# One transfer for all but the last 392 nodes, issued behind the last load, and the last group's remainder rows first

## The chip, the cores and the metric

The kernel runs on one core of a Trainium2 chip. Its time is device microseconds (us), a median over runs. An execution taken by the hardware profiler gives the span (first to last instruction) and the trace. TensorE is PE, VectorE is DVE, ScalarE is ACT, GpSimd is POOL, SyncE is SP. Transfers issued by SP run as queue q1 and those issued by ACT as queue q10. One trace shows both on the core's 16 DMA engines. KB is 1024 bytes, MB and GB are powers of ten.

## What is computed

One layer over 5000 nodes with 64 features, float32:

```python
h = jnp.maximum(_layernorm(x, axis=-1), 0.0)
neighbors = adj @ h                                   # adj is 5000 x 5000
neighbors = neighbors / (num_neighbors[:, None] + 1e-7)
out = jnp.concatenate([h, neighbors], axis=-1) @ fc_w.T + fc_b
return x + relu(out)
```

The 5000 x 5000 matrix is 100 MB and every element of it is read once.

## The kernel before

The host gives the kernel adj transposed, with its columns (the nodes whose sums are wanted) in three groups of 2048, 2560 and 392. `GROUPS` holds them as (first block of 512, blocks, first accumulator). The kernel multiplies h by the neighbour half of `fc_w` first, which gives `g_sb` (128 rows x 40 tiles x 64), so that the big product is g^T times a tile of adj: 64 output rows on one half of the TensorE array, and two halves side by side.

Contraction runs over 5000 source nodes: 39 tiles of 128, and a remainder of 8 rows (`REM`). For each group in turn, `LOADS` lists the transfers of 1 to 4 tiles each, 40 in all. SP issues them in that order into a ring `raw` of 128 x 32768 floats, and waits on `load_used` before it reuses a place. TensorE takes tile after tile in `multiply` (line 611) and accumulates into the banks of the group: `acc[0]`, `acc[1]` for the group of 2048, `acc[2]` to `acc[4]` for that of 2560, and the bank `turned` (which is `acc[5]`) for the last 392 columns. A place in this order is written (group, tile).

The 8 remainder rows of a group are loaded by ACT into `adj_rem`, every 16th lane (`REM_STEP`), and multiplied in `remainder` (line 624) behind the tile that `REM_AFTER` names. Lanes between them hold zeros from a memset on GpSimd (line 279). The first group's rows are loaded early; those of the second wait for `rem_used` of the first and are issued at 116.6 us; those of the last group wait for the second's.

When a group is summed, VectorE scales its banks by 1/neighbours (`scale`, `scale_alone`), TensorE flips them back to nodes x features in `flip` at the places of `FLIP_AFTER`, into the two banks `y[0]` and `y[1]`, and VectorE adds what h contributes by itself and then x (`finish`). `out_ready` counts the banks finished. The last 392 nodes have a shorter way: `preload_self` (line 647, behind tile (2, 25)) puts their own part into `y[0]` and `y[1]` by a product with the identity, once `out_ready` is 5. Behind the last tile come `scale_last`, `flip_last` (line 653), which adds to the same banks, and `finish_last` (line 526).

There are three stores of the output. ACT issues the one of the first group (512 KB, pieces of 1 KB) when `out_ready` is 2, and the one of the second (640 KB, pieces of 1.25 KB) when it is 5 (line 358). SP issues the one of the last 392 nodes (98 KB, line 268) behind all loads, when `out_ready` is 6. A piece is what lies together in memory: a lane of `out_sb` holds 36 nodes that are neighbours in the output, and a group takes 4 or 5 out of each 9 of them. The kernel ends when both engines have seen their stores land.

Of the kernel before, what the change touches and what calls it, by code (L numbers as in the profile page):

```python
# [18 lines left out]

LANDINGS = 24  # L20

REM_STEP = 16
REM_GAP = 8
LN_EPS = 1e-5
DIV_EPS = 1e-7
# [14 lines left out]
def gnn_layer(nc, x, adj_groups, num_neighbors, fc_t, fc_b, out):  # L40
# [64 lines left out]
    TURN_AFTER = {(0, 3): 1, (0, 7): 2, (0, 13): 3, (0, 21): 4}  # L105
    WEIGH_AFTER = {(0, 5): 1, (0, 11): 2, (0, 19): 3, (0, 27): 4}
    SPREAD_AFTER = (0, 38)
    REM_AFTER = {(0, 33): 0, (1, 11): 1, (2, 3): 2}
    FLIP_AFTER = {(1, 7): 0, (1, 9): 1, (2, 9): 2, (2, 13): 3, (2, 17): 4}
    PRELOAD_AFTER = (2, 25)  # L110
    LN_OPS = 8

    REM_LOADS = [sum(1 + (w > BLOCK and w % (2 * BLOCK) > 0) for w in WIDTH[:g + 1]) for g in range(G)]

    with ExitStack() as ctx:
        def sb(name, shape, dt=F32):
# [9 lines left out]
        g_sb = sb("g_sb", [LANES, TILES, F])  # L126
        cen = sb("cen", [LANES, BT * F])
        h_pairs = [sb(f"h_pairs{i}", [LANES, BT * F]) for i in range(2)]
        ht = [sb(f"ht{i}", [LANES, BLOCK]) for i in range(2)]
        ht_rows = sb("ht_rows", [LANES, 2 * SIDE])  # L130
        ht_rem = sb("ht_rem", [LANES, LANES])
# [33 lines left out]
        bias_copied = sem("bias_copied")  # L165
        landed = [sem(f"landed{k}") for k in range(LANDINGS)]
        rem_loaded = sem("rem_loaded")
        ln_dve = sem("ln_dve")
        ln_act = sem("ln_act")
        ident_cleared = sem("ident_cleared")  # L170
# [30 lines left out]
        def nodes(v, m0, m1):  # L201

            return v[0:TAIL0, :].rearrange("(p i m) f -> p i (m f)", i=RUN, m=FULL)[:, :, m0 * F:m1 * F]

        def tail(v):

# [34 lines left out]
        @block.sync  # L241
        def _(sp):
            def load(n):
                g, m, i0, i1 = LOADS[n]
                w = WIDTH[g]
                if loads_before(n):
                    sp.wait_ge(load_used, loads_before(n))
                r = RUN if m < FULL else TAIL_RUN
                rows = adj_groups[g][m * BLOCK:m * BLOCK + r * LANES, 0:w].rearrange("(p i) c -> p (i c)", i=r)
                sp.dma_start(raw[:, place(n):place_end(n)], rows[:, i0 * w:i1 * w]).then_inc(loaded(n)[0], 16)  # L250

            def load_x(k):
# [36 lines left out]
        def _(act):  # L289
            def load_rem(g):  # L290
                w = WIDTH[g]
                if g:
                    act.wait_ge(rem_used, g)
                else:
                    act.wait_ge(rem_cleared, 2)
                rows = adj_groups[g][REM0:N, 0:w]
                lanes = slice(0, REM * REM_STEP, REM_STEP)
                k = w // (2 * BLOCK) * 2
                if k:
                    act.dma_start(adj_rem[lanes, 0:k, 0:BLOCK],  # L300
                                  rows[:, 0:k * BLOCK].rearrange("r (k c) -> r k c", k=k)).then_inc(rem_loaded, 16)
                if w > k * BLOCK:
                    act.dma_start(halves(adj_rem[lanes, k, :])[:, :, 0:(w - k * BLOCK) // 2],
                                  rows[:, k * BLOCK:w].rearrange("r (s c) -> r s c", s=2)).then_inc(rem_loaded, 16)

            def load_few():

# [47 lines left out]
            def store(g):  # L355
                m0, m1 = GROUPS[g][0], GROUPS[g + 1][0]
                act.wait_ge(out_ready, banks(g)[-1] + 1)
                act.dma_start(nodes(out, m0, m1), blocks(out_sb, m0, m1)).then_inc(stored, 16)


            act.wait_ge(warm_ready, 1)
            nc.scalar.activation(std[:, 0:1], warm[:], ACT.Sqrt)
# [13 lines left out]
            for b in range(SETS):  # L376
                copy_spread(b)
            load_rem(1)
            store(0)
            load_rem(2)  # L380
            store(1)
            act.wait_ge(stored, 32)

        @block.vector
        def _(dve):
# [46 lines left out]
            def add_bias(b):  # L432
                if b == 0:
                    dve.wait_ge(bias_spread, 1)
                    nc.vector.tensor_copy(bias[:], acc[ALONE][:, 0:F]).then_inc(bias_copied, 1)
# [86 lines left out]
            def finish_last():  # L522

                for i in range(2):
                    dve.wait_ge(flipped, LAST + i + 1)
                    done = nc.vector.scalar_tensor_tensor(
                        tail_half(out_sb, i), y[i][0:LAST_LANES, 0:2 * F].rearrange("p (s f) -> p s f", s=2), 0.0,
                        tail_half(x_sb, i), ALU.max, ALU.add)
                done.then_inc(out_ready, 1)

# [26 lines left out]
        def _(pe):  # L557
# [47 lines left out]
            def multiply(n, i):  # L605
# [3 lines left out]
                for b in banks(g):  # L609
                    for s, c0, width in sides(g, b):  # L610
                        last = nc.tensor.matmul(acc[b][s * HALF:(s + 1) * HALF, 0:width], g_sb[:, t, :],  # L611
                                                raw[:, c + c0:c + c0 + width], start=t == 0, stop=t == CH - 1,
                                                tile_position=(0, s * HALF))
                if i == i1 - 1:
                    last.then_inc(load_used, 1)

            def remainder(g):
                pe.wait_ge(rem_loaded, 16 * REM_LOADS[g])
                for b in banks(g):
                    for s, c0, width in sides(g, b):  # L620
                        k = adj_rem[:, c0 // BLOCK, 0:BLOCK]
                        if width < BLOCK:
                            k = halves(adj_rem[:, (c0 - s * width) // BLOCK, :])[:, s, 0:width]
                        last = nc.tensor.matmul(acc[b][s * HALF:(s + 1) * HALF, 0:width], g_sb[:, CH, :], k,  # L624
                                                start=False, stop=False, tile_position=(0, s * HALF))
                last.then_inc(rem_used, 1)

            def flip(b):
# [13 lines left out]

            def preload_self():

                pe.wait_ge(out_ready, LAST)
                for i in range(2):
                    nc.tensor.matmul(y[i][0:LAST_LANES, 0:2 * F].rearrange("p (s f) -> p s f", s=2),
                                     ident[0:LAST_LANES, 0:LAST_LANES], tail_half(out_sb, i), start=True, stop=False)

            def flip_last():  # L650
                for i in range(2):
                    pe.wait_ge(scaled, LAST + i + 1)
                    nc.tensor.matmul(y[i][0:LAST_LANES, 0:2 * F], sums[0][:, i * LAST_LANES:(i + 1) * LAST_LANES],
                                     ident[:], start=False, stop=True).then_inc(flipped, 1)


            pe.wait_ge(bias_loaded, 16)
            pe.wait_ge(bias_cleared, 2)
            nc.tensor.matmul(acc[ALONE][:, 0:F], ones[:], bias_row[:], start=True, stop=True).then_inc(bias_spread, 1)  # L659
            pe.wait_ge(ident_ready, 1)  # L660
            turn(0)
            pe.wait_ge(weights_loaded, 32)
# [53 lines left out]
```

## Time and profile before

| | |
|---|---|
| time, median of 3 runs | 250.93 us (250.77 to 251.14) |
| profiled execution: its own time | 250.9 us |
| profiled execution: its span | 249.1 us |
| PE busy | 207.5 us (83%) |
| DVE, ACT, POOL busy | 41.3, 15.2, 3.7 us |
| DMA, bytes and mean rate | 102.79 MB, 413 GB/s |
| mean granted clock of TensorE | 0.959 |

The profiled execution's time is 1.8 us above its span; that part lies around the instructions. In the rows below a share of DMA time is a share of 16 engines for the length of the window: 10% of a window of 8 us is 0.8 us in which all 16 would be taken. A matmul in float32 counts as two instructions on TensorE, so a tile of the first group has 8, one of the second 12, one of the last 4.

### The profile page before, as it was taken

To read this page: it belongs to the slowest core of one execution; us is meant where nothing else is said; L and a number is where in the kernel's file an instruction comes from. 1 tells how busy PE (TensorE), PEld (TensorE's weight loads), DVE (VectorE), ACT (ScalarE), POOL (GpSimd) and SP (SyncE) were. 2 spreads that over 40 slices of the span, in tenths; PEclk is the share of its full clock that TensorE was granted. 3 is DMA by queue.
4 is the path that set the end of the run, shared out by engine and by line. 5 is a ranking of instruction groups with operands and counts; after the bars stand their busy time and mean duration, and the time that the engine had idled before them with its cause. 6 is when DMAs were issued, how large, how long until landed. Compare 5 with 4: busy or idle time off the path is not lost.

```text
span 249.1 us, 2445 instructions
## 1 busy us (share of the span) xinstructions
PE 207.5 (83%) x1084; PEld 86.2 (35%) x1084; DVE 41.3 (17%) x101; ACT 15.2 (6%) x35; POOL 3.7 (1%) x13
## 2 busy tenths in 40 slices
PE   0279899688997997998995299997398998798994
PEld 0143333322432442332332033332132433235782
DVE  1762333330020050006002001000000000003411
ACT  2130220120020010003000000000000000000000
POOL 5000000000000000000000000000000000000000
PEclk9999999997999999999999579999769999999999
DMA  8999999999999999999999999999999999999992
GB/s 294 411 431 421 427 421 421 432 424 414 418 426 453 437 442 389 441 428 431 399 429 441 441 434 400 430 457 431 434 431 407 424 424 424 421 415 417 417 395 71
DMA packets 8309, 102.79 MB, mean 413 GB/s; under 512 B 1412, under 2 KB 3244, under 8 KB 4972
## 3 DMA queue, kind: packets, MB, share of 16 engines
q1 hardware_dynamic: 6754, 101.29, 96.1%
q10 hardware_dynamic: 1546, 1.36, 1.6%
q8 instruction: 8, 0.13, 0.2%
q14 instruction: 1, 0.01, 0.0%
HBM read 101.37 MB, written 1.28 MB: 412 GB/s over the span
## 4 chain that ended last, share of the span: by engine, by line
DMA 66%; PE 29%; DVE 2%; ACT 1%; SPq 1%; issue 1%
DMA raw<-adj_group 64%; PE acc L611 24%; DMA x_sb<-x 2%; PE acc L624 2%; PE y L576 2%; PE turned L611 1%; SPq L250 1%; PE turned L564 0%; DVE cen L426 0%; DVE cen L414 0%; DVE var L418 0%; DVE mean L407 0%; ACT g_sb L348 0%; ACT sums L322 0%; ACT ht L342 0%
## 5 line engine op out<-in xcount | busy, mean ns | idle before, releaser
L611 PE MATMUL acc<-raw,g_sb 128*64 128x512 f32 (+1 forms) x780 | 162.8, 573 | 25.3 <-DMA raw<-adj_group 24.4
L611 PEld LDWEIGHTS acc<-raw,g_sb 128*64 128x64 f32 x780 | 56.5, 142 | 125.2 <-issue 90.2
L492 DVE TENSOR_TENSOR sums<-acc,rnn_bc 128x512 f32<-128x512 f32 x4 | 2.6, 686 | 78.6 <-PE acc L611 76.6
L611 PE MATMUL turned<-raw,g_sb 128*64 128x196 f32 x156 | 14.8, 334 | 0.9 <-DMA raw<-adj_group 0.8
L576 PE MATMUL y<-w_both,ht 128*128 128x256 f32 (+1 forms) x40 | 12.1, 440 | 0.8 <-ACT ht L342 0.8
L611 PEld LDWEIGHTS turned<-raw,g_sb 128*64 128x64 f32 x156 | 10.5, 136 | 4.2 <-DMA raw<-adj_group 2.1
L442 DVE TENSOR_TENSOR out_sb<-y,bias 128x128 f32<-128x128 f32 x20 | 4.4, 284 | 38.2 <-ACT g_sb L348 38.2
L576 PEld LDWEIGHTS y<-w_both,ht 128*128 128x128 f32 x40 | 8.0, 217 | 5.6 <-issue 4.4
L518 DVE TENSOR_TENSOR out_sb<-y,out_sb 128x512 f32<-128x512 f32 (+1 forms) x5 | 3.2, 639 | 33.9 <-PE y L637 32.8
L463 DVE TENSOR_TENSOR rnn_diag<-ident,rnn 128x512 f32<-128x512 f32 x8 | 5.0, 686 | 19.6 <-PE y L601 19.6
L564 PE MATMUL turned<-ident,h_pairs 128*128 128x128 f32 x20 | 3.7, 315 | 4.6 <-DVE h_pairs L430 4.6
L418 DVE TENSOR_REDUCE var<-sums 128x8 f32<-128x512 f32 x5 | 3.4, 686 | 16.3 <-ACT sums L322 16.3
L659 PE MATMUL acc<-bias_row,ones 128*128 128x64 f32 x2 | 0.7, 448 | 6.2 <-DMA bias_row<-fc_b 6.2
L348 ACT ACTIVATE g_sb<-y 128x256 f32<-128x256 f32 x10 | 3.3, 381 | 41.2 <-PE y L576 26.3
L601 PE MATMUL y<-rnn_diag,ones 128*64 128x512 f32 (+1 forms) x20 | 4.6, 552 | 0.8 <-ACT rnn_bc L353 0.7
L564 PEld LDWEIGHTS turned<-ident,h_pairs 128*128 128x128 f32 x20 | 2.4, 156 | 8.0 <-issue 7.2
L353 ACT ACTIVATE rnn_bc<-y 128x512 f32<-128x512 f32 (+1 forms) x5 | 2.9, 587 | 25.1 <-PE y L601 25.1
L407 DVE TENSOR_REDUCE mean<-x_sb 128x8 f32<-128x512 f32 (+1 forms) x6 | 3.5, 590 | 4.9 <-DMA x_sb<-x 4.9
L624 PE MATMUL acc<-adj_rem,g_sb 128*64 128x512 f32 (+1 forms) x20 | 4.2, 550 | 0.0
L342 ACT ACTIVATE ht<-turned 128x512 f32<-128x512 f32 x5 | 3.0, 597 | 19.5 <-PE turned L564 19.5
L414 DVE TENSOR_TENSOR cen<-x_sb,mean 128x512 f32<-128x512 f32 (+1 forms) x6 | 3.5, 602 | 0.2
L322 ACT ACTIVATE sums<-cen 128x512 f32<-128x512 f32 x5 | 3.1, 626 | 7.0 <-DVE cen L414 6.0
(56 smaller groups left out, 41.3 us busy)
## 6 DMA issues: line engine op xcount, KB each, us to landing
raw<-adj_group SPq DMA_DIRECT2D x9, 4096.0 KB, 31.8
raw<-adj_group SPq DMA_DIRECT2D x5, 5120.0 KB, 26.7
raw<-adj_group SPq DMA_DIRECT2D x8, 2560.0 KB, 27.6
raw<-adj_group SPq DMA_DIRECT2D x7, 784.0 KB, 27.3
raw<-adj_group SPq DMA_DIRECT2D x3, 1280.0 KB, 21.2
raw<-adj_group SPq DMA_DIRECT2D x1, 3072.0 KB, 28.3
raw<-adj_group SPq DMA_DIRECT2D x4, 392.0 KB, 19.1
x_sb<-x SPq DMA_DIRECT2D x2, 576.0 KB, 4.7
```

The lines of the kernel that those rows point to most:

```text
L348: nc.scalar.activation(to[:, 2 * k:2 * k + 2, :, :], weighed_parts(k, 1), ACT.Copy).then_inc(g_copied, 1)
L407: last = nc.vector.tensor_reduce(narrow(mean[:]), rows, AX_X, ALU.add)
L414: last = nc.vector.tensor_tensor(wide(cen[:]), rows, m.unsqueeze(len(m.shape)).to_broadcast(list(rows.shape)), ALU.subtract)
L418: nc.vector.tensor_reduce(var[:], sums[0][:].rearrange("p (t f) -> p t f", f=F), AX_X, ALU.add).then_inc(ln_dve, 1)
L442: last = nc.vector.tensor_tensor(to[:, 2 * k:2 * k + 2, :], weighed_parts(k, 0)[:, :, s, :], bias[:].unsqueeze(1).to_broadcast([LANES, 2, ...
L463: last = nc.vector.tensor_tensor(split(to[:, s, :]), ident[:].unsqueeze(1).to_broadcast(shape), rnn[:, m + s:ROWS:FULL].unsqueeze(2).to_br ...
L518: nc.vector.tensor_tensor(o, split(y[b % 2][:, 0:RUN * F * (m1 - m0)]), o, ALU.add).then_inc(summed, 1)
L564: last = nc.tensor.transpose(turned[:, c], h_pairs[b % 2][:, c], ident[:])
L576: last = nc.tensor.matmul(weighed_tiles(i)[:, 0:w], ht[b % 2][:, c:c + LANES], flat(w_both[:])[:, 0:w], start=True, stop=True)
L601: last = nc.tensor.matmul(y[b % 2][k, c], ones[:, 0:HALF], r, start=True, stop=True, tile_position=(0, s * HALF))
L611: last = nc.tensor.matmul(acc[b][s * HALF:(s + 1) * HALF, 0:width], g_sb[:, t, :], raw[:, c + c0:c + c0 + width], start=t == 0, stop=t == ...
L624: last = nc.tensor.matmul(acc[b][s * HALF:(s + 1) * HALF, 0:width], g_sb[:, CH, :], k, start=False, stop=False, tile_position=(0, s * HALF))
```

## The change

The two stores on ACT become one on SP, issued behind the last load when `out_ready` is 5: 1152 KB, in which each lane is one piece of 9216 bytes. The store of the last 392 nodes goes from SP to ACT. The remainder rows of the last group get a tile of their own (`adj_rem_last`, which is `h_pairs[1]` after its last use, cleared on GpSimd), are loaded by ACT right behind those of the second group, and are multiplied behind tile (1, 23), where they open the accumulation; the first tile of the last group then adds to it. `preload_self` goes from tile (2, 25) to (1, 19), waits for the scaling of the first group's two banks, and writes `acc[0]` and `acc[1]` in place of `y[0]` and `y[1]`; `flip_last` and `finish_last` use these too. The remainder rows lie in every 4th lane. The bias is spread through `acc[SETS - 1]`, which is the same bank as before (`ALONE` is 4 and `SETS` is 5).

```diff
-REM_STEP = 16
+REM_STEP = 4
...
-    REM_AFTER = {(0, 33): 0, (1, 11): 1, (2, 3): 2}
+    REM_AFTER = {(0, 33): 0, (1, 11): 1, (1, 23): 2}
...
-    PRELOAD_AFTER = (2, 25)
+    PRELOAD_AFTER = (1, 19)
...
+        adj_rem_last = h_pairs[1]
...
-            sp.wait_ge(out_ready, LAST + 1)
-            sp.dma_start(tail_nodes(out), tail(out_sb)).then_inc(last_stored, 16)
-            sp.wait_ge(last_stored, 16)
+
+            sp.wait_ge(out_ready, LAST)
+            sp.dma_start(out[0:TAIL0, :].rearrange("(p r) f -> p (r f)", r=ROWS), flat(out_sb[:, 0:ROWS, :])
+                         ).then_inc(stored, 16)
+            sp.wait_ge(stored, 16)
...
+            pool.wait_ge(ones_ready, 3)
+            pool.wait_ge(turned_done, SETS - 1)
+            nc.gpsimd.memset(adj_rem_last[:], 0.0).then_inc(rem_cleared, 1)
...
                 if g:
-                    act.wait_ge(rem_used, g)
+                    act.wait_ge(rem_used, 1)
...
+                if g == 1:
+                    act.wait_ge(rem_cleared, 3)
+                    act.dma_start(halves(adj_rem_last[lanes, :])[:, :, 0:SIDE],
+                                  adj_groups[G - 1][REM0:N, :].rearrange("r (s c) -> r s c", s=2)).then_inc(rem_last_loaded, 16)
...
             load_rem(1)
-            store(0)
-            load_rem(2)
-            store(1)
-            act.wait_ge(stored, 32)
+            act.wait_ge(out_ready, LAST + 1)
+            act.dma_start(tail_nodes(out), tail(out_sb)).then_inc(last_stored, 16)
+            act.wait_ge(last_stored, 16)
...
-                                                raw[:, c + c0:c + c0 + width], start=t == 0, stop=t == CH - 1,
+                                                raw[:, c + c0:c + c0 + width], start=g < G - 1 and t == 0, stop=t == CH - 1,
...
             def preload_self():
 
-                pe.wait_ge(out_ready, LAST)
+                pe.wait_ge(scaled, 2)
                 for i in range(2):
-                    nc.tensor.matmul(y[i][0:LAST_LANES, 0:2 * F].rearrange("p (s f) -> p s f", s=2),
+                    nc.tensor.matmul(acc[i][0:LAST_LANES, 0:2 * F].rearrange("p (s f) -> p s f", s=2),
                                      ident[0:LAST_LANES, 0:LAST_LANES], tail_half(out_sb, i), start=True, stop=False)
```

## Rows read from the trace of the kernel before

**Rows 1.** The page, parts 2 and 3: busy tenths in 40 slices; the DMA queues.

```profile
DMA  8999999999999999999999999999999999999992
...
q1 hardware_dynamic: 6754, 101.29, 96.1%
q10 hardware_dynamic: 1546, 1.36, 1.6%
```

**Rows 2.** The chain of waits from 200 us to the end: start us, us, what.

```profile
224.86 2.37 PE acc L611 x12
...
229.35 15.57 DMA raw<-adj_group
...
244.97 0.58 PE turned L611 x4
...
246.38 0.51 DVE out_sb L526 x2
```

**Rows 3.** DMA queues, 195 to 236 us, no store under way.

```profile
DMA packets 1853, 17.33 MB, mean 423 GB/s; under 512 B 207, under 2 KB 207, under 8 KB 1080
```

**Rows 4.** DMA queues, 150.7 to 192.4 us, the first store: issue KB, us to landing.

```profile
q10 hardware_dynamic: 546, 0.53, 3.7%
...
out<-out_sb ACTq DMA_DIRECT2D x1, 512.0 KB, 41.6
```

**Rows 5.** DMA queues, 237.6 to 245.2 us, the second store.

```profile
q10 hardware_dynamic: 528, 0.66, 23.4%
...
out<-out_sb ACTq DMA_DIRECT2D x1, 640.0 KB, 7.6
```

**Rows 6.** DMA queues, 243 to 245 us, the last loads.

```profile
q10 hardware_dynamic: 211, 0.25, 34.3%
q1 hardware_dynamic: 40, 0.05, 6.6%
```

**Rows 7.** Timeline of TensorE from 165 us: start us, us, instructions, idle time before.

```profile
178.69 11.66 PE L611 MATMUL acc<-raw,g_sb 128*64 128x512 f32 x48 [5.67 <-DMA raw<-adj_group]
191.24 17.41 PE L611 MATMUL acc<-raw,g_sb 128*64 128x512 f32 x96 [0.89 <-DMA raw<-adj_group]
209.47 4.52 PE L611 MATMUL acc<-raw,g_sb 128*64 128x512 f32 x24 [0.82 <-DMA raw<-adj_group]
215.57 8.81 PE L611 MATMUL acc<-raw,g_sb 128*64 128x512 f32 x48 [1.58 <-DMA raw<-adj_group]
224.86 2.37 PE L611 MATMUL acc<-raw,g_sb 128*64 128x512 f32 x12 [0.48 <-DMA raw<-adj_group]
...
228.39 0.50 PE L624 MATMUL turned<-adj_rem,g_sb 128*64 128x196 f32 x4
228.72 1.52 PE L611 MATMUL turned<-raw,g_sb 128*64 128x196 f32 x16
230.63 0.88 PE L611 MATMUL turned<-raw,g_sb 128*64 128x196 f32 x8 [0.38 <-DMA raw<-adj_group]
...
239.41 0.68 PE L647 MATMUL y<-out_sb,ident 98*98 98x128 f32 x4
240.02 4.57 PE L611 MATMUL turned<-raw,g_sb 128*64 128x196 f32 x48
```

**Rows 8.** Timeline, the last store's issue.

```profile
246.92 0.40 SPq L268 DMA_DIRECT2D out<-out_sb  x1
```

**Rows 9.** Windows behind it, columns: PEclk, DMA share, GB/s come last.

```profile
247.50:248.00 0.50, 0.00 (x0) 0.00 (x0) 0.00 (x0) 0.00 (x0) 0.00 (x0) 1.00 0.32 85
...
248.50:249.10 0.60, 0.00 (x0) 0.00 (x0) 0.00 (x0) 0.00 (x0) 0.00 (x0) 1.00 0.00 0
```

**Rows 10.** The line of the two stores on ACT: duration ns min/median/max.

```profile
L358 ACTq DMA_DIRECT2D out<-out_sb x2: 602/622/641, 150.7 to 237.6; - x2
```

**Rows 11.** Line of the last remainder loads: duration ns min/median/max, first and last start.

```profile
L303 ACTq DMA_DIRECT2D adj_rem<-adj_group x2: 616/627/638, 117.3 to 155.9; - x2
```

**Rows 12.** Line of the memset on GpSimd, the same columns.

```profile
L279 POOL MEMSET adj_rem<- x1: 2264/2264/2264, 1.6 to 1.6; 128x2600 f32 x1
```

More of the change, by code:

```diff
@@ L107, in gnn_layer @@
     SPREAD_AFTER = (0, 38)
-    REM_AFTER = {(0, 33): 0, (1, 11): 1, (2, 3): 2}
+    REM_AFTER = {(0, 33): 0, (1, 11): 1, (1, 23): 2}
     FLIP_AFTER = {(1, 7): 0, (1, 9): 1, (2, 9): 2, (2, 13): 3, (2, 17): 4}
-    PRELOAD_AFTER = (2, 25)
+    PRELOAD_AFTER = (1, 19)
     LN_OPS = 8
-    REM_LOADS = [sum(1 + (w > BLOCK and w % (2 * BLOCK) > 0) for w in WIDTH[:g + 1]) for g in range(G)]
+    REM_LOADS = [sum(1 + (w % (2 * BLOCK) > 0) for w in WIDTH[:g + 1]) for g in range(G - 1)]
     with ExitStack() as ctx:
@@ L167, in gnn_layer @@
         rem_loaded = sem("rem_loaded")
+        rem_last_loaded = sem("rem_last_loaded")
         ln_dve = sem("ln_dve")
@@ L199, in blocks @@
             return v[:, 0:ROWS, :].rearrange("p (i m) f -> p i (m f)", m=FULL)[:, :, m0 * F:m1 * F]
-        def nodes(v, m0, m1):
-            return v[0:TAIL0, :].rearrange("(p i m) f -> p i (m f)", i=RUN, m=FULL)[:, :, m0 * F:m1 * F]
         def tail(v):
@@ L298, in load_rem @@
                 k = w // (2 * BLOCK) * 2
-                if k:
-                    act.dma_start(adj_rem[lanes, 0:k, 0:BLOCK],
-                                  rows[:, 0:k * BLOCK].rearrange("r (k c) -> r k c", k=k)).then_inc(rem_loaded, 16)
+                act.dma_start(adj_rem[lanes, 0:k, 0:BLOCK],
+                              rows[:, 0:k * BLOCK].rearrange("r (k c) -> r k c", k=k)).then_inc(rem_loaded, 16)
                 if w > k * BLOCK:
-                    act.dma_start(halves(adj_rem[lanes, k, :])[:, :, 0:(w - k * BLOCK) // 2],
+                    act.dma_start(halves(adj_rem[lanes, k, :])[:, :, 0:BLOCK // 2],
                                   rows[:, k * BLOCK:w].rearrange("r (s c) -> r s c", s=2)).then_inc(rem_loaded, 16)
+                if g == 1:
+                    act.wait_ge(rem_cleared, 3)
+                    act.dma_start(halves(adj_rem_last[lanes, :])[:, :, 0:SIDE],
+                                  adj_groups[G - 1][REM0:N, :].rearrange("r (s c) -> r s c", s=2)).then_inc(rem_last_loaded, 16)
             def load_few():
@@ L353, in copy_spread @@
                 nc.scalar.activation(rnn_bc[:, b, 0:w], y[b % 2][:, 0:w], ACT.Copy).then_inc(spread_copied, 1)
[L355 to L358, printed above, removed]
             act.wait_ge(warm_ready, 1)
@@ L434, in add_bias @@
                     dve.wait_ge(bias_spread, 1)
-                    nc.vector.tensor_copy(bias[:], acc[ALONE][:, 0:F]).then_inc(bias_copied, 1)
+                    nc.vector.tensor_copy(bias[:], acc[SETS - 1][:, 0:F]).then_inc(bias_copied, 1)
                     dve.wait_ge(bias_copied, 1)
@@ L526, in finish_last @@
                     done = nc.vector.scalar_tensor_tensor(
-                        tail_half(out_sb, i), y[i][0:LAST_LANES, 0:2 * F].rearrange("p (s f) -> p s f", s=2), 0.0,
+                        tail_half(out_sb, i), acc[i][0:LAST_LANES, 0:2 * F].rearrange("p (s f) -> p s f", s=2), 0.0,
                         tail_half(x_sb, i), ALU.max, ALU.add)
@@ L617, in remainder @@
             def remainder(g):
-                pe.wait_ge(rem_loaded, 16 * REM_LOADS[g])
+                if g < G - 1:
+                    pe.wait_ge(rem_loaded, 16 * REM_LOADS[g])
+                else:
+                    pe.wait_ge(rem_last_loaded, 16)
                 for b in banks(g):
                     for s, c0, width in sides(g, b):
-                        k = adj_rem[:, c0 // BLOCK, 0:BLOCK]
-                        if width < BLOCK:
-                            k = halves(adj_rem[:, (c0 - s * width) // BLOCK, :])[:, s, 0:width]
+                        if width == BLOCK:
+                            k = adj_rem[:, c0 // BLOCK, 0:BLOCK]
+                        else:
+                            k = adj_rem[:, (c0 - s * width) // BLOCK, :] if b == ALONE else adj_rem_last[:]
+                            k = halves(k)[:, s, 0:width]
                         last = nc.tensor.matmul(acc[b][s * HALF:(s + 1) * HALF, 0:width], g_sb[:, CH, :], k,
-                                                start=False, stop=False, tile_position=(0, s * HALF))
+                                                start=g == G - 1, stop=False, tile_position=(0, s * HALF))
                 last.then_inc(rem_used, 1)
@@ L652, in flip_last @@
                     pe.wait_ge(scaled, LAST + i + 1)
-                    nc.tensor.matmul(y[i][0:LAST_LANES, 0:2 * F], sums[0][:, i * LAST_LANES:(i + 1) * LAST_LANES],
+                    nc.tensor.matmul(acc[i][0:LAST_LANES, 0:2 * F], sums[0][:, i * LAST_LANES:(i + 1) * LAST_LANES],
                                      ident[:], start=False, stop=True).then_inc(flipped, 1)
@@ L658, in _ @@
             pe.wait_ge(bias_cleared, 2)
-            nc.tensor.matmul(acc[ALONE][:, 0:F], ones[:], bias_row[:], start=True, stop=True).then_inc(bias_spread, 1)
+            nc.tensor.matmul(acc[SETS - 1][:, 0:F], ones[:], bias_row[:], start=True, stop=True).then_inc(bias_spread, 1)
             pe.wait_ge(ident_ready, 1)
```

## The prediction

> **What bounds the kernel now.** I read the page first. Of its DMA line the reader is to see that every slice but the first and the last is at 9, and that the two queues together hold 97.7% of the 16 engines' span [rows 1]. The kernel is a transfer of 102.79 MB with everything else beside it, so a change pays by taking bytes out of the stream, or by shortening what follows the last load. Next the chain of waits: it ends with a load that lands at 244.92 (229.35 + 15.57), four matmuls of one tile to 245.54, and at 246.38 the last VectorE work, which ends at 246.89 [rows 2]. So behind the last load there are 1.97 us of computing, and then a store to the end of the span at 249.1.
>
> Then the queues, by windows. Where no store is under way the stream moves 423 GB/s [rows 3]. The first store of 512 KB is issued at 150.7 and takes 41.6 us to land; in its window queue q10 holds 3.7% of 41.7 us, which is 1.54 us of all 16 engines [rows 4]. The second, 640 KB, has 23.4% of 7.6 us, which is 1.78 us [rows 5]. Both stand in front of loads that the end waits for. One thing at the end is not plain: from 243 to 245 us the loads' queue has only 6.6% (40 packets) and the store's queue 34.3% [rows 6]. Most engines had no load left by 243, and a few late ones still had both. The end waits for the late ones.
>
> **What the change takes off the loads.** The two stores leave the time before the last load: 1.54 + 1.78 = 3.32 us of all engines. The stream was full in both windows, so I take all of it for the loads: the last lands at 244.92 - 3.32 = 241.60. Bounds: if the late engines had been rid of only part of the second store's work (the 34.3% of the last 2 us is 0.69 us on engines that may already have had no load), it is 1.54 + 1.78 - 0.69 = 2.63 us, so 242.3. A gain of more than 3.32 is shut off by TensorE, as follows.
>
> **TensorE in the tail.** The last load of the second group arrives at 224.86; with only the first store before it, 1.54 earlier, at 223.32. Its 12 matmuls take 2.37, to 225.69. From 227.23 to 245.54 TensorE worked on the last group, 18.31 us. In it are two waits of 0.38 for loads, at 230.63 and at 244.97 (the gap behind 240.02 + 4.57 = 244.59) [rows 7]. Two pieces of work go from there: the remainder, whose net time is the step from one row to the next, 228.72 - 228.39 = 0.33, and the preload, 240.02 - 239.41 = 0.61 [rows 7]. What is left is 18.31 - 0.76 - 0.33 - 0.61 = 16.61, and so TensorE can't end before 225.69 + 16.61 = 242.30. By the loads it ends at 241.60 + 0.05 + 0.57 = 242.22. The two bounds meet; the later, 242.30, is 3.24 before 245.54. If TensorE had no more load to wait for, faster DMA would bring nothing.
>
> **Where the moved TensorE work goes.** The preload, 0.68 busy, lands behind tile (1, 19), ahead of the 5.67 us that TensorE waits for a load at 178.69. The remainder, 0.50, lands behind (1, 23), at 190.35, in a wait of 0.89. That wait shrinks as the first store goes: tile (1, 24) can come at 189.7, and TensorE then is 0.50 + 0.65 late. Three later waits, 0.82, 1.58 and 0.48, sum 2.88, take this up [rows 7]: from 190.85 with 17.41 busy it is at 208.26 against an arrival at 207.93, and from there, with 4.52, at 212.78 against 214.03. Nothing is left over at 223.32. So both edits cost nothing on the path; uncovered, they would cost 1.2 us. The flips stay behind the same tiles, with the same VectorE work between them.
>
> **Behind the last tile.** From 245.54 to 246.89 is 1.35: 242.30 gives 243.65. SP issued the last store at 246.92 in 0.40 us [rows 8], and the span ends 2.18 after that. Packets fill 32% of 247.5 to 248.0 and none are seen after 248.5 [rows 9], so some 0.8 us go before the first packet and 0.6 behind the last. On ACT an issue takes 0.60 to 0.64 [rows 10], 0.2 more. So: 243.68 + 2.18 + 0.2 = 246.06.
>
> **The large store.** It waits for `out_ready` 5, which came at 237.6 [rows 10] and now comes at some 235.4 (1.54 for the load, 0.71 for the remainder and a wait that are gone), with loads still queued: it is behind them in q1 on each engine and delays none. SP has nothing behind it. 1152 KB are 1.18 MB. At the loads' rate it takes 2.79 us [rows 3]; at that of the second store, 0.66 MB in 1.78 us, 3.18; at that of the first, 0.53 in 1.54, 3.43 [rows 4, 5]. The rate grows with the piece, and these pieces are of 9 KB, so I take 3.0. The upper bound is the last store's: 0.10 MB within 1.0 us [rows 9] would make it 11.8. With 3.0 its last packet is at 244.6 and it is seen at 245.2. The last store's packets begin at 244.7, just behind. So the large store is seen 0.9 before the end, and costs nothing.
>
> How long a store is unseen behind its last packet is 0.6 us in the rows [rows 9], and the sum goes by that. The Trainium skill (DMA: Bandwidth & Descriptors, Anatomy of one DMA) fits some 2.0 us of fixed time to each transfer (on another issue path), most of it the receipt of the last write and heaviest for HBM, and its rules advise to issue early so that this overlaps. No row here shows 2.0; by that rule the large store would end at 246.6 and be the last, an estimate of 248.4 us, which is a part of rival 1.
>
> **The rest.** The remainder rows of the last group were issued at 155.9 and now at about 117.9, 0.6 us of ACT, which waits for nothing there; they are wanted at 190 [rows 11]. The lanes 4 apart, the same bytes in as many pieces: nothing, or a few tenths of a transfer that has over 30 us. The memset on GpSimd is 512 of columns where 2600 took 2.26 us [rows 12], so 0.45 (an estimate by size) at a time when GpSimd has no other work, and some 70 us before it is wanted. If VectorE were held up by it, that is 0.45 us in a part where DMA sets the pace. The bias goes through the same bank. ACT waits for the end without work behind it.
>
> **Sum.** Span 249.1 - 246.06 = 3.04 less. The profiled execution's time is 250.9, which is the median of the runs shown to 0.03, so 250.9 - 3.04 = 247.9. I add 0.1 for packets of the two stores that meet: 248.0.
>
> **Rivals.**
>
> 1. *The large store ends the kernel.* For it: the engines that end their loads late have all 8 of their pieces still before them, and the small store's packets share these engines. From 242.3 with 3.43 us it is done at 245.7, seen at 246.3, and with the small store's packets squeezed in behind it the end is 0.5 to 1.5 later, 246.8 to 247.8: 248.6 to 249.6 us. Against it: 0.6 us is what the rows show. Chance 0.2.
>
> 2. *TensorE is late.* At half the clock (1.2 GHz) 48 matmuls take longer: 11.66 us from 178.69, where the same 48 took 8.81 from 215.57 [rows 7]. If such a stretch came again behind 190 us, in a stream with earlier loads, TensorE would be 2.85 + 1.15 late against 2.88 of waits: 1.1 us at the end, 249.1 us. For it: the waits shrink. Against it: before, this happened behind waits of over 5 us, and the one behind 173 shrinks. Chance 0.05.
>
> 3. *The loads don't come earlier*, since the stores took engines that were waiting anyway. The last lands at 244.92 still, the large store is seen at 244.92 + 3.0 + 0.6 = 248.5, and the small one, on ACT, 0.2 later than before: 251.1 us, no change. For it: the share of the last 2 us is far from full [rows 6]. Against it: from 150 us on the share is at its top with the stores in it. Chance 0.06.
>
> 4. *Slower: writes alone run slowly.* Nothing in the trace shows a large store by itself; the last store, alone, moved 0.10 MB in 1.0 us. At this rate the large one ends at 241.6 + 11.8 + 0.6 = 254.0, which is 255.8 us. It decides once the store takes over 6.9 us (241.6 to 248.5), under 171 GB/s. Against it: that store had pieces of 512 bytes, and two earlier ones ran at 344 and 371 GB/s amid loads. Chance 0.08.
>
> **How the numbers follow.** Forecast, 0.61: 248.0 us, own range 247.5 to 248.6. Rival 1 (0.2) reaches 249.6 and rival 2 lies inside it. With 0.14 in rivals 3 and 4 outside and a little below 247.5, the range for 8 in 10 is 247.4 to 249.6. A measurement can tell 0.2% here, 0.5 us. Faster: the forecast and rivals 1 and 2, 0.86. Same: rival 3, 0.06. Slower: 0.08.
>
> **What the profile after would show.** In 150 to 192 us q10 nearly gone. The chain's last load lands at 241.6 (242.3 at most) and TensorE's waits among the last group's tiles are near nothing. One issue of 1152 KB on SP near 235.4, with q1 over 90% busy until some 244.5. The issue of 98 KB on ACT near 243.7, taking 0.6, and the end 2.4 us behind it. The preload at 173 and the remainder at 190, both ahead of a wait for a load. The prediction is wrong if the last load still lands at 244 or later, if the large store's packets go on past 245.5, or if TensorE has 1 us of work left when the last load lands.

## The result and the profile after

The changed kernel takes 247.64 us (247.62 to 247.82, 4 runs) against 251.03 (250.77 to 251.14, 4 runs): ratio 0.9868, 95% interval 0.9851 to 0.9885. The profiled execution took 247.82 us with a span of 246.0, 3.1 us less than before; 248.0 was predicted, and a span of 246.06. By the medians the fall is 3.39 us, where 2.9 was predicted (250.9 to 248.0).

The page, parts 2 and 3, against [rows 1]:

```profile
DMA  8899999999999999999999999999999999999995
...
DMA packets 7397, 102.79 MB, mean 418 GB/s; under 512 B 1396, under 2 KB 2204, under 8 KB 3932
...
q1 hardware_dynamic: 6688, 102.37, 98.0%
q10 hardware_dynamic: 700, 0.28, 0.4%
```

The bytes are the same. The store queue q10 shrank from 1.36 to 0.28 MB, and the last slice of the DMA line, 2 before, is 5.

The end of the chain of waits, against [rows 2] (start us, us, what):

```profile
228.73 0.04 issue
228.78 0.88 PE turned L612 x8
...
234.82 5.46 PE turned L612 x64
...
240.29 2.12 PE turned L612 x20
...
242.43 0.27 DVE sums L510
...
243.25 0.51 DVE out_sb L527 x2
```

Before, the chain ran through one load to 244.92 and then one tile. Now it seems to be TensorE's own work from 228.78 on, to the end of the last tile at 242.41, 3.13 us earlier. TensorE's timeline, against [rows 7]:

```profile
139.82 7.24 PE L612 MATMUL acc<-raw,g_sb 128*64 128x512 f32 x24 [6.23 <-DMA raw<-adj_group]
...
171.37 0.68 PE L654 MATMUL acc<-out_sb,ident 98*98 98x128 f32 x4
177.16 11.64 PE L612 MATMUL acc<-raw,g_sb 128*64 128x512 f32 x48 [5.12 <-DMA raw<-adj_group]
188.64 0.50 PE L631 MATMUL turned<-h_pairs,g_sb 128*64 128x196 f32 x4
189.29 17.41 PE L612 MATMUL acc<-raw,g_sb 128*64 128x512 f32 x96 [0.15 <-DMA raw<-adj_group]
207.59 4.52 PE L612 MATMUL acc<-raw,g_sb 128*64 128x512 f32 x24 [0.90 <-DMA raw<-adj_group]
213.69 8.81 PE L612 MATMUL acc<-raw,g_sb 128*64 128x512 f32 x48 [1.58 <-DMA raw<-adj_group]
222.97 2.37 PE L612 MATMUL acc<-raw,g_sb 128*64 128x512 f32 x12 [0.46 <-DMA raw<-adj_group]
...
226.84 1.55 PE L612 MATMUL turned<-raw,g_sb 128*64 128x196 f32 x16 [0.18 <-DMA raw<-adj_group]
228.78 0.88 PE L612 MATMUL turned<-raw,g_sb 128*64 128x196 f32 x8 [0.38 <-DMA raw<-adj_group]
...
234.75 7.63 PE L612 MATMUL turned<-raw,g_sb 128*64 128x196 f32 x84
```

The preload stands at 171.37 ahead of a wait of 5.12, the remainder at 188.64 ahead of one of 0.15. The last wait for a load is at 228.78, and here the view misleads, since the ends of matmuls are modelled. The weight loads that go ahead of the matmuls show what each tile waited for:

```profile
234.75 5.17 PEld L612 LDWEIGHTS turned<-raw,g_sb 128*64 128x64 f32 x64
240.29 0.86 PEld L612 LDWEIGHTS turned<-raw,g_sb 128*64 128x64 f32 x12 [0.36 <-DMA raw<-adj_group]
241.33 0.20 PEld L612 LDWEIGHTS turned<-raw,g_sb 128*64 128x64 f32 x4 [0.18 <-DMA raw<-adj_group]
241.83 0.20 PEld L612 LDWEIGHTS turned<-raw,g_sb 128*64 128x64 f32 x4 [0.30 <-DMA raw<-adj_group]
```

The last tiles wait again (a tile is four of these instructions), and the last load is seen at 241.83 where it was 244.96 before (the second fence, with 0.73 of waiting), 3.13 us earlier:

```profile
244.96 0.20 PEld L611 LDWEIGHTS turned<-raw,g_sb 128*64 128x64 f32 x4 [0.73 <-DMA raw<-adj_group]
```

So the loads still set the end, with TensorE close behind them. There is also a row that the prediction has no term for: the load that TensorE waited for at 141.42 before came at 139.82, and no store had been issued yet in either kernel:

```profile
141.42 7.23 PE L611 MATMUL acc<-raw,g_sb 128*64 128x512 f32 x24 [7.03 <-DMA raw<-adj_group]
```

The two stores: SyncE's waits, then the line of the small store and windows of the end (PEclk, DMA share, GB/s last), against [rows 8, 9]:

```profile
SPq L115 <- DMA out<-out_sb: 8.4, 1, 8.4
...
SPq L115 <- PEq L115: 1.3, 1, 1.3
```

```profile
235.77 0.35 SPq L268 DMA_DIRECT2D out<-out_sb  x1
```

```profile
L382 ACTq DMA_DIRECT2D out<-out_sb x1: 353/353/353, 243.8 to 243.8; - x1
```

```profile
243.00:243.50 0.50, 0.43 (x4) 0.21 (x2) 0.25 (x2) 0.00 (x0) 0.00 (x0) 1.00 0.14 55
243.50:244.00 0.50, 0.00 (x0) 0.00 (x0) 0.26 (x2) 0.00 (x0) 0.00 (x0) 1.00 0.09 37
244.00:244.50 0.50, 0.00 (x0) 0.00 (x0) 0.00 (x0) 0.00 (x0) 0.00 (x0) 1.00 0.00 0
244.50:245.00 0.50, 0.00 (x0) 0.00 (x0) 0.00 (x0) 0.00 (x0) 0.00 (x0) 1.00 0.53 142
```

The large store is issued at 235.77, and SyncE sees it 8.4 us after that instruction's end, at 244.5. No packet moves between 244.0 and 244.5: the large store was done before the small one, issued at 243.79, began. Then SyncE waits 1.3 us for the others. So it was hidden with 1.3 us to spare.

### The profile page after: what moved, and what is told of

Read it like the earlier page. It is cut to its first block, busy times and chain, and to the rows that moved or that the text cites. A ratio compares the mean times of both kernels' runs of the same rounds, so it can differ in the third digit from the quotient of the medians.

```text
span 246.0 us, 2446 instructions
## 1 busy us (share of the span) xinstructions
PE 207.9 (85%) x1084; PEld 86.3 (35%) x1084; DVE 41.3 (17%) x101; ACT 15.2 (6%) x35; POOL 4.2 (2%) x14
## 4 chain that ended last, share of the span: by engine, by line
DMA 60%; PE 35%; DVE 2%; ACT 1%; issue 1%; SPq 0%
DMA raw<-adj_group 58%; PE acc L612 25%; PE turned L612 5%; DMA x_sb<-x 2%; PE acc L631 2%; PE y L577 2%; PE y L644 1%; PE turned L565 0%; PE y L646 0%; DVE cen L415 0%; DVE cen L427 0%; DVE var L419 0%; DVE mean L408 0%; ACT g_sb L355 0%; ACT sums L329 0%
```

## The experiments

All were timed in turn with the kernel before, on the same chip within each group of four. The kernel before had medians of 251.15 (first group), 251.01 (second) and 251.07 (third). The changed kernel's 247.64 was measured with 251.03.

### The lanes alone, undone

```diff
 # changed kernel
-REM_STEP = 4
+REM_STEP = 16
```

> The changed kernel with the remainder rows in every 16th lane again, nothing else. In the two traces, loads already came 0.7 us earlier at 96 us and 1.6 us earlier at 140 us, before any store had been issued. Theory A (the step of the lanes does this: writing 8 rows to lanes 16 apart holds up a few engines, and the stream goes at the pace of the latest): arrivals at 96 and 140 us fall back to 96.8 and 141.4, and the time is 0.7 to 1.6 us above the changed kernel, 248.4 to 249.3 us. Theory B (the lanes cost nothing, the early lead is a difference between two executions): 247.6 us, arrivals within 0.3 us of the changed kernel or scattered.

Measured: 248.63 us (248.52 to 248.74), ratio 0.9901 (0.9887 to 0.9914). Undoing the lanes costs 1.0 us. Arrivals are at 96.57 and 141.69: theory A.

### The lanes alone, done

```diff
 # kernel before
-REM_STEP = 16
+REM_STEP = 4
```

> The kernel before with the remainder rows in every 4th lane, nothing else. Theory A (the step of the lanes): 249.4 to 250.3 us, with the load at 141.4 us coming at about 139.8. Theory B (lanes cost nothing): 251.0 us, arrivals as before.

Measured: 250.08 us (249.99 to 250.26), ratio 0.9959 (0.9946 to 0.9971), 1.07 us faster. The wait at 141.42 ends at 140.45, not at 139.8. One trace is a rough measure here: over all runs with these rows loaded, this load comes at 139.82 to 140.98 with lanes 4 apart (eight traces, mean 140.4) and at 141.09 to 141.80 otherwise (five traces, mean 141.5). The ranges don't touch, and the lead is some 1.1 us where the first two traces had 1.6. What moved in the queues between 110 and 140 us, first in the kernel before, then in this one:

```profile
DMA packets 556, 12.55 MB, mean 418 GB/s; under 512 B 75, under 2 KB 91, under 8 KB 123
...
q1 hardware_dynamic: 491, 12.45, 98.4%
```

```profile
DMA packets 573, 13.04 MB, mean 435 GB/s; under 512 B 80, under 2 KB 96, under 8 KB 128
...
q1 hardware_dynamic: 508, 12.94, 100.6%
```

The kernel before has its engines 2% less busy for the loads and moves 4% less. This is the stretch in which the 80 KB of the second group's remainder rows are loaded. The lanes' undoing and the next experiment (both 16 apart) give 12.52 and 12.55 MB, like the kernel before.

### The stores alone

```diff
 # kernel before, SyncE
-            sp.wait_ge(out_ready, LAST + 1)
-            sp.dma_start(tail_nodes(out), tail(out_sb)).then_inc(last_stored, 16)
-            sp.wait_ge(last_stored, 16)
+            sp.wait_ge(out_ready, LAST)
+            sp.dma_start(out[0:TAIL0, :].rearrange("(p r) f -> p (r f)", r=ROWS), flat(out_sb[:, 0:ROWS, :])
+                         ).then_inc(stored, 16)
+            sp.wait_ge(stored, 16)
 # ScalarE: both stores out, the last one in
             load_rem(1)
-            store(0)
             load_rem(2)
-            store(1)
-            act.wait_ge(stored, 32)
+            act.wait_ge(out_ready, LAST + 1)
+            act.dma_start(tail_nodes(out), tail(out_sb)).then_inc(last_stored, 16)
+            act.wait_ge(last_stored, 16)
```

> The kernel before with the stores of the change alone: one transfer of 1152 KB behind the loads from SyncE, the last store from ScalarE; lanes, remainder and preload as before. By the prediction's sum the stores alone bring the last load to 241.6, but TensorE has 0.94 us more to do in the tail and ends at 243.2: about 248.9 us. If the lanes are worth 0.9 to 1.6 us (theory A) and stores only the rest, it comes out at 248.6 to 249.4 us as well, but with the load at 141.4 us where it was; if the stores alone make the whole change, 247.7 us.

Measured: 248.82 us (248.64 to 249.02), ratio 0.9908 (0.9895 to 0.9922): 2.33 us of the 3.4. The wait at 141.42 ends at 141.09, among the traces without lanes 4 apart (141.09 to 141.80), so the early lead isn't there. TensorE's last tile ends at 243.33, with the preload and the remainder in the tail:

```profile
235.43 2.80 PE turned L612 x32
238.24 0.61 PE y L648 x4
238.85 4.49 PE turned L612 x52
...
243.36 0.27 DVE sums L510
```

Here the weight loads of the last tiles show no wait for a load at all (52 in one piece, as in the run below with TensorE's work put back): with this work in the tail, TensorE does set the end.

### No large store

```diff
 # changed kernel, SyncE: the first 4608 nodes aren't written
-            sp.wait_ge(out_ready, LAST)
-            sp.dma_start(out[0:TAIL0, :].rearrange("(p r) f -> p (r f)", r=ROWS), flat(out_sb[:, 0:ROWS, :])
-                         ).then_inc(stored, 16)
-            sp.wait_ge(stored, 16)
```

> The changed kernel without the store of the first 4608 nodes; only the last 392 are written. If the large store is hidden behind the last computing (the forecast), the time stays at 247.5 to 247.7 us. If it delays the last load, or the small store, or the end (rival 1), the time falls by what it costs, 0.3 us or more.

Measured: 247.69 us (247.54 to 247.76), the changed kernel's time. 1.18 MB of writes at the end cost nothing that can be measured. Rival 1 of the prediction, and rival 4 with it, are out.

With no store in the way, the windows of this run's trace also show how the loads end (PEclk, DMA share, GB/s last):

```profile
239.00:240.00 1.00, 1.00 (x16) 0.67 (x10) 0.00 (x0) 0.00 (x0) 0.00 (x0) 1.00 0.85 314
240.00:241.00 1.00, 0.95 (x14) 0.69 (x12) 0.00 (x0) 0.00 (x0) 0.00 (x0) 1.00 0.38 138
241.00:242.00 1.00, 1.00 (x14) 0.48 (x10) 0.00 (x0) 0.00 (x0) 0.00 (x0) 1.00 0.02 6
```

From 238 to 239 the loads' queue still has 100.0% of the 16 engines. Then it runs empty, and the last load is seen only at 241.75. So the last load waits for engines that are still at work while others have nothing left to load, as the prediction suspected [rows 6]. From 239 to 241 this leaves 0.15 + 0.62, some 0.8 us of all engines, unused (an estimate from these rows). How the work lies on single engines isn't shown, for a window gives the mean of the 16.

### The first store early again

```diff
 # changed kernel; SyncE stores only blocks 4 to 8 behind the loads, in the form of the kernel before
+            act.wait_ge(out_ready, GROUPS[1][2])
+            act.dma_start(nodes(out, 0, GROUPS[1][0]), blocks(out_sb, 0, GROUPS[1][0])).then_inc(first_stored, 16)
```

> The changed kernel with the first group's store (512 KB) taken out of the large one and issued by ScalarE as soon as that group is finished, as before; SyncE stores the rest behind the loads in pieces of 1.25 KB. Theory 1 (a store costs the loads its share of the queues): 1.54 us, of which TensorE's hold on the tail gives back nothing, 249.2 us. Theory 2 (from the arrivals of the runs so far: the load of the second group's end came at 223.6 and 223.9 without the first store and at 224.9 with it): 1.0 to 1.1 us, 248.7 us. Theory 3 (stores in the middle cost nothing): 247.7 us.

Measured: 249.01 us (248.97 to 249.47), ratio 0.9924 (0.9912 to 0.9937): 1.37 us slower than the changed kernel, between theories 1 and 2. But 0.3 of this lies outside the span: the time is 2.07 to 2.11 above the span in all five runs of this kernel, and 1.7 to 1.9 in every other. The reason isn't shown; this kernel has one semaphore and one wait more than the changed kernel. The span has a median of 246.9, where the changed kernel's are 245.8 to 246.0. That is some 1.05 us, theory 2. The load of the second group's end comes at 224.16 where it came at 222.97.

### TensorE's work back in the tail

```diff
 # changed kernel
-    REM_AFTER = {(0, 33): 0, (1, 11): 1, (1, 23): 2}
+    REM_AFTER = {(0, 33): 0, (1, 11): 1, (2, 3): 2}
-    PRELOAD_AFTER = (1, 19)
+    PRELOAD_AFTER = (2, 25)
 # and start=t == 0 for tiles, start=False for the remainder
```

> The changed kernel with the last remainder and the preload back behind tiles (2, 3) and (2, 25), their loads and banks as changed. If TensorE sets the end of the tail, as the trace after shows (no wait for a load after 228.8 us), this adds 0.33 + 0.61 less what a wait of 0.38 takes up and less what the loads leave: 0.2 to 0.9 us, 247.9 to 248.5 us. If the loads set it, 247.7 us.

Measured: 248.22 us (247.91 to 248.36), 0.58 more than the changed kernel; the ranges of the runs don't touch. In its trace the load of the second group's end comes at 223.21, against 222.97; such a difference is within the scatter of single traces (222.60 to 223.21 in six that do the same with their loads up to there). Behind it, TensorE ends 19.73 us later (at 242.94), against 19.44: 0.29 us in the tail. The weight loads before the end show one row of 52 without a wait, against the three waits of the changed kernel:

```profile
238.38 4.18 PEld L612 LDWEIGHTS turned<-raw,g_sb 128*64 128x64 f32 x52
```

So with 0.94 us more to do in the tail, TensorE is late. The same pair exists with lanes 16 apart: the stores alone (248.82, TensorE's work in the tail) and the lanes undone (248.63, that work moved). There the moves are worth 0.19 us in time, with ranges that overlap, and 0.31 in the tail (19.73 against 19.42).

### The large store in small pieces

```diff
 # changed kernel, SyncE
-            sp.dma_start(out[0:TAIL0, :].rearrange("(p r) f -> p (r f)", r=ROWS), flat(out_sb[:, 0:ROWS, :])
-                         ).then_inc(stored, 16)
-            sp.wait_ge(stored, 16)
+            for m0, m1 in ((0, GROUPS[1][0]), (GROUPS[1][0], FULL)):
+                sp.dma_start(nodes(out, m0, m1), blocks(out_sb, m0, m1)).then_inc(stored, 16)
+            sp.wait_ge(stored, 32)
```

> The changed kernel with the large store as two, both on SyncE behind the loads, in pieces of 1 KB and 1.25 KB as before, in place of one with pieces of 9 KB. By the queue's shares before, 3.3 us in place of 3.0 for the large one, which is hidden: 247.7 us. If small pieces hold the last loads or the small store back, 248 us or more.

Measured: 247.68 us (247.53 to 247.84), no change. The one transfer and its long pieces are worth nothing that can be measured; what counts is its place behind the loads.

### The flips earlier

```diff
 # changed kernel
-    FLIP_AFTER = {(1, 7): 0, (1, 9): 1, (2, 9): 2, (2, 13): 3, (2, 17): 4}
+    FLIP_AFTER = {(1, 7): 0, (1, 9): 1, (2, 3): 2, (2, 7): 3, (2, 11): 4}
```

> The changed kernel with the three flips of the second group behind tiles (2, 3), (2, 7) and (2, 11) in place of (2, 9), (2, 13) and (2, 17). In the trace after, TensorE waits 0.18 and 0.38 us for loads at 226.8 and 228.8 us, ahead of the flips, and never again until the end. If TensorE sets the end, a flip in each wait brings up to 0.56 us, as far as the last load (seen near 241.7) allows, about 0.3 to 0.5: 247.1 to 247.4 us. If the loads set the end, 247.6 us. If a flip then waits for VectorE, it is slower.

Measured: 247.61 us (247.48 to 247.93), no change. The two waits ahead of the flips are gone, and the weight loads wait in their place at 236.48 and 239.43, and then as in the changed kernel:

```profile
236.48 2.52 PEld L612 LDWEIGHTS turned<-raw,g_sb 128*64 128x64 f32 x32 [0.72 <-DMA raw<-adj_group]
239.43 0.53 PEld L612 LDWEIGHTS turned<-raw,g_sb 128*64 128x64 f32 x8 [0.43 <-DMA raw<-adj_group]
240.39 0.86 PEld L612 LDWEIGHTS turned<-raw,g_sb 128*64 128x64 f32 x12 [0.43 <-DMA raw<-adj_group]
241.43 0.20 PEld L612 LDWEIGHTS turned<-raw,g_sb 128*64 128x64 f32 x4 [0.18 <-DMA raw<-adj_group]
241.93 0.20 PEld L612 LDWEIGHTS turned<-raw,g_sb 128*64 128x64 f32 x4 [0.30 <-DMA raw<-adj_group]
```

Freeing TensorE brought nothing, for the loads set the end; giving it 0.94 us more to do made it late.

### The rows in lanes 0 to 7

```diff
 # changed kernel
-REM_STEP = 4
+REM_STEP = 1
```

> The changed kernel with the 8 remainder rows in lanes 0 to 7. Between 110 and 140 us, where the second group's remainder rows are loaded, the three traces with lanes 16 apart moved 12.52 to 12.55 MB and the three with lanes 4 apart 12.93 to 13.04. Theory P (what costs is that rows share a port into the memory: the Trainium skill, SBUF, puts each four lanes in a row on one port, so that lanes 16 apart use 4 ports and lanes 4 apart 8): lanes 0 to 7 use two ports, and it is no better than lanes 16 apart: 248.6 us or more, at most 12.6 MB. Theory Q (only far-apart lanes cost, whatever the reason): 247.6 us, some 12.95 MB.

Measured: 248.85 us (248.79 to 249.0), ratio 0.991 (0.9895 to 0.9924). Theory Q falls: the nearest lanes are no better than the farthest. The bytes were not as theory P had them, 12.77 MB and not 12.6 at most, but the load that ends the wait came at 141.80, as late as with lanes 16 apart.

### The rows in every 8th lane

```diff
 # changed kernel
-REM_STEP = 4
+REM_STEP = 8
```

> The changed kernel with the rows in every 8th lane (0 to 56). Theory P: these are 4 ports with two rows each, as with lanes 16 apart: 248.6 us, 12.5 MB between 110 and 140 us. Theory Q (distance): between the two, about 247.9 to 248.3 us.

Measured: 248.72 us (248.58 to 249.31), ratio 0.9908 (0.9893 to 0.9923), and 12.52 MB, both as with lanes 16 apart:

```profile
DMA packets 579, 12.52 MB, mean 417 GB/s; under 512 B 83, under 2 KB 115, under 8 KB 147
```

### No remainder rows loaded

```diff
 # changed kernel, ScalarE: the 8 source nodes are left out of the sums; TensorE waits for the cleared tiles alone
-                act.dma_start(adj_rem[lanes, 0:k, 0:BLOCK], ...
-                    act.dma_start(halves(adj_rem[lanes, k, :])[:, :, 0:BLOCK // 2], ...
-                    act.dma_start(halves(adj_rem_last[lanes, :])[:, :, 0:SIDE], ...
```

> The changed kernel with no remainder row loaded (the tiles stay zero, so these 8 source nodes are left out of the sums); the remainder's matmuls still run. If lanes 4 apart leave no cost but the bytes (0.16 MB on a part of the engines), the time is 247.3 to 247.6 us; if the loads of the rows still hold up the stream, 247.2 us or less, as far as TensorE lets it.

Measured: 247.19 us (247.01 to 247.26), 0.45 less than the changed kernel. Spread over the stream's rate of [rows 3], 0.16 MB are 0.38 us, so little but bytes is left to gain there.

### Flips earlier, and the last loads of one tile each

```diff
 # changed kernel, with the flips as above; the last of these three rows of STEPS
-(4, 4, 4, 4, 4, 4, 4, 2, 2, 1)]
+(4, 4, 4, 4, 4, 4, 4, 2, 1, 1)]
```

> The changed kernel with the flips behind (2, 3), (2, 7), (2, 11), and the last load of two tiles split into one each. Moving the flips alone gave 247.6 us, no change: TensorE waited at 236.5 for what it had saved, and again worked through the last five tiles, 2.12 us, from the arrival of the two-tile load at 240.35. If that load's arrival sets the end, its first half comes some 0.2 to 0.4 us earlier: 247.2 to 247.5 us. If the last single tile sets it (seen near 241.7, and one tile takes 0.4), 247.6 us.

Measured: 247.73 us (247.59 to 247.82), no change. The edit splits both loads of two tiles, not only the last, so each of the last seven tiles comes by itself. The weight loads tell why it brings nothing:

```profile
236.04 2.85 PEld L612 LDWEIGHTS turned<-raw,g_sb 128*64 128x64 f32 x36 [0.71 <-DMA raw<-adj_group]
...
239.62 0.20 PEld L612 LDWEIGHTS turned<-raw,g_sb 128*64 128x64 f32 x4 [0.33 <-DMA raw<-adj_group]
240.11 0.20 PEld L612 LDWEIGHTS turned<-raw,g_sb 128*64 128x64 f32 x4 [0.29 <-DMA raw<-adj_group]
240.61 0.20 PEld L612 LDWEIGHTS turned<-raw,g_sb 128*64 128x64 f32 x4 [0.30 <-DMA raw<-adj_group]
241.12 0.20 PEld L612 LDWEIGHTS turned<-raw,g_sb 128*64 128x64 f32 x4 [0.31 <-DMA raw<-adj_group]
241.63 0.20 PEld L612 LDWEIGHTS turned<-raw,g_sb 128*64 128x64 f32 x4 [0.32 <-DMA raw<-adj_group]
```

TensorE waits for every one of the last tiles, and they come 0.5 us apart. A tile of the last group is 128 x 392 x 4 bytes, 0.20 MB, so this is 400 GB/s, about the rate of the queues. Neither smaller loads nor a freer TensorE helped: what is left is the pace at which the last loads land. That isn't the pace of 16 full engines, as the windows of the run without the large store show. Spreading the last loads more evenly over the engines, worth some 0.8 us at most by that estimate, was not tried.

## Why the prediction was right, and where it was lucky

The time, 248.0 against 247.64, and the sign were right, and the mechanism that was put forward is real: the stores go behind the last load and are free there. That the numbers meet so closely is luck. The sum's 3.04 us of span against 3.1 measured agrees better than its terms do, and the pair of profiled executions flatters it: the one before was among the faster of its kernel (250.9), the one after the slowest of its four (247.82). With the lanes undone, the median falls by 2.52 us (251.15 to 248.63). That is what all but the lanes is worth, where the forecast has 2.9; the lanes, which the prediction has at nothing, bring the rest. The last load of the second group marks a border that all traces have; what comes before it is the stream, what comes after is the tail.

| | predicted, us | measured, us |
|---|---|---|
| stream: first store | 1.54 | 0.95 to 1.26: 224.86 against 223.91 and 223.60 (lanes 16 apart); 1.19: 224.16 against 222.97 (lanes 4 apart) |
| stream: lanes | 0 | 0.9: 224.86 against 223.96 (first store early), 223.91 against 222.97 (first store gone) |
| stream, together | 1.54 | 1.89 |
| tail: second store, from the border to the last load | 1.78 | 1.24: 20.10 against 18.86 |
| last load seen, together | 3.32 | 3.13 |
| TensorE's end | 3.24 | 3.13 |

The tail's figure is steady. From the border to the last load are 20.10 and 20.16 us in the two kernels with the second store early (the kernel before, and the lanes alone done), and 18.78 to 18.87 in nine with that store behind the loads or left out; with the two-tile loads split it is 19.03, and the other two have no wait at the last load. The stream's figures are less sure: the border itself lies anywhere from 222.60 to 223.21 in six traces of the changed kernel's stream, so they are good to some 0.3 us. The times and spans bear them out: lanes 1.07 and 0.99, first store some 1.05.

*The step that failed* is the sentence on "the lanes 4 apart, the same bytes in as many pieces: nothing". They are worth 1.0 us, a third of the whole, shown from both sides: 1.07 alone and 0.99 undone. Both stores' terms, 1.54 and 1.78, were too large, by 0.3 to 0.6 and by 0.54. The three errors have opposite signs and partly cancel; without that, 2.5 us would have stood against 2.9.

*What a store costs the loads.* The working multiplied the store queue's share by the window, which is the time in which its packets held engines. What the loads lose is less, 60 to 80% of it (1.24 of 1.78; 0.95 to 1.26 of 1.54). The prediction's lower bound of 2.63 had a reason for this: in the last 2 us before, the queue shares were 34.3 and 6.6% [rows 6], and part of the second store could run on engines with no load left. The run without the large store bears it out, for there some 0.8 us of engine time is unused before the last load. 1.78 - 0.69 = 1.09 was that bound, and 1.24 lies just above it. For the first store, in the middle, the reason is open. Its whole price, by putting it back, was 1.37 us in time and some 1.05 in span; in the traces the last load was then seen at 243.03 against 241.83, 1.20 later.

*TensorE in the tail.* "The two bounds meet" was roughly right: the loads set the end, and TensorE has some 0.65 us to spare (0.94 - 0.29). With its 0.94 us back in the tail, TensorE had no wait and ended 19.73 us after the border arrived (17.55 + 2.37 = 19.92 by the prediction's rows, perhaps because matmul rows hide short waits), and 0.29 later than with the loads in the lead. So the moves of preload and remainder are worth 0.3 in the tail once the stores are gone, 0.2 and 0.6 in time in the two pairs, and nothing, by its wait of 0.73 for the last load, in the kernel before (not run by itself).

*Moved work.* The preload lies ahead of 5.12 us of waiting, as predicted. The remainder leaves 0.15 of the 0.89, and the waits of 0.90, 1.58 and 0.46 behind it show that TensorE had caught up.

*The large store.* Issued at 235.8 (predicted 235.4), done before 244.0 (244.6), seen at 244.5 (245.2): all of it hidden, rivals 1 and 4 out by the run without it. Rival 2 didn't come: the mean granted clock was 0.972 (0.959 before), and the 48 matmuls from 213.69 take 8.81 us, as before. The slow stretch that the rival was modelled on came again at its old place, 11.64 us from 177.16. In both kernels its mean granted clock was 0.75: in the kernel before 0.50 up to 182 and 1.00 from 186 on, so only a part of it ran at 1.2 GHz, where the rival speaks of half the clock. Rival 3 is out by the stores alone. The Trainium skill's 2.0 us of fixed time (DMA: Bandwidth & Descriptors, Anatomy of one DMA), fitted on another issue path, don't agree with this case: it puts most of them behind the last write, and the large store was seen 0.5 to 1.0 us after its last packet (some are in the window to 244.0, none later; seen at 244.5).

*Behind the last tile.* Predicted 1.35 + 0.03 + 2.38 = 3.76. Measured 246.0 - 242.41 = 3.6, mostly because the issue took 0.35 us on ScalarE and not 0.6.

**What lanes cost.** A remainder transfer writes 8 rows into 8 lanes. The times group by how these lanes lie: every 4th 247.64, every 16th 248.63, every 8th 248.72, the first eight 248.85. Distance doesn't order them. The Trainium skill (SBUF — State Buffer, Door 1: The DMA port swizzle) gives four neighbouring lanes, and the four that are 32 further, one port of 16: by it the rows use 8 ports in the first case, 4 in the second and third, 2 in the last, and the order of the times agrees, with 248.72 and 248.85 too close to tell apart. For two of these runs it gave the times before they ran; the bytes of the last case, 12.77 MB, were not what it gave. What isn't shown is whether rows that share a port are slow, or rows that land on a port which another engine's part of the big loads is using: each pattern here that avoids the one avoids the other. Nor is it shown why 80 KB hold up a stream of 12.9 MB by 0.4 MB.

No run with the whole work in it beats the changed kernel by more than can be measured: 247.61, 247.68 and 247.73 against 247.64.

## What to carry to other kernels

Where the DMA queues are full to the end, a store is worth its place more than its form: ahead of the last load each of these cost about 1 us, behind it 1.18 MB were free, for the last tiles' computing and the small store's 2.2 us covered them. Before trusting a sum that comes out right, compare arrival times at a few fixed loads, also ahead of the first place that the sum speaks of: here a lead of some 1.1 us was there before any store. A single pair of traces gave 1.6 for it, so read such a lead from several runs. And a mean share near full doesn't say that the last load lands with full engines: here their mean share fell to 85 and then 38% in the last two us of loading. A change of a constant that says which lanes a small transfer writes isn't free by its bytes: time it by itself.

## What the hardware showed that I had not expected

- 8 rows written to lanes 16, 8 or 1 apart instead of 4 cost 1.0 to 1.2 us over the kernel, with the same bytes. Between 110 and 140 us the traces at 8 and 16 apart moved 12.52 to 12.55 MB, that at 1 12.77, those at 4 12.93 to 13.05.
- An issue's time went more with the transfer's form than with the engine. The output's store in four pieces a lane took 0.60 to 0.64 us on ScalarE [rows 10] and, in the run with the first store early, 0.61 on SyncE:

```profile
236.94 0.61 SPq L274 DMA_DIRECT2D out<-out_sb  x1
```

  With one piece a lane it took 0.35 on SyncE, and the small store took 0.40 on SyncE [rows 8] and 0.35 on ScalarE. The form isn't all: the same store with one piece a lane took 0.78 on SyncE in the last experiment, and the second of two issued back to back took 1.33 where the first took 0.62 (the large store in small pieces). Why is open.
- A row of matmuls can hide waits. In the changed kernel the last five tiles stand as 20 matmuls in one busy piece of 2.12 us, 0.42 a tile, where four tiles take 1.48 (0.37) when their data is there. The chain of waits put this down to TensorE. The weight loads showed waits of 0.36, 0.18 and 0.30 in it, and these decided which resource ended the kernel.
